# Attention with an FFN before and behind it on one core: order round the first scores and the fourth block, and A11 and A12 of FFN pair 2 turned by DMA

## What is computed

```python
x = L0_attn_x                                   # 2 x 1024 x 512, fp32
x = x + 0.5 * ffn(layernorm(x))
x = x + attention(layernorm(x))
x = x + 0.5 * ffn(layernorm(x))                 # same weights as above
# ffn: (silu(x @ Wg) * (x @ Wu)) @ Wd, 512 -> 1376 -> 512, weights from 4-bit groups
# attention: one head of 128, q k v = x @ Wqkv + b; softmax(q k^T / sqrt(128)) v @ Wo + bo
```

## Time and profile before

| | us |
|---|---|
| median of 3 runs | 828.96 (828.56 to 829.65) |
| the profiled execution | 829.12 |
| its span, first to last instruction | 827.3 |
| TensorE busy in it | 808.2 |

### The profile page before, as it was taken

How to read it: one execution, slowest core, us unless ns; L and a number is a source line. 1 busy time by engine, 2 the same in 40 slices (tenths; PEclk the granted TensorE clock), 3 DMA queues, 4 the chain that set the end, 5 groups by cost and what they waited for, 6 DMA issues and landing times. The chain is left out here.

```text
span 827.3 us, 10465 instructions
## 1 busy us (share of the span) xinstructions
PE 808.2 (98%) x3836; PEld 663.0 (80%) x3836; DVE 493.6 (60%) x801; ACT 273.0 (33%) x469; POOL 297.9 (36%) x235
## 2 busy tenths in 40 slices
PE   5999999999999999999998999999999999999998
PEld 4777778878888888787886888888878788888786
DVE  7899945766554543563756896545347744443452
ACT  3333433455211211432754872121123311211221
POOL 5556614652115363335754362064431210110100
PEclk9999999999999999999999999999999999999999
DMA  5998968975754467348183058735968155344121
GB/s 162 283 336 276 317 190 278 336 267 229 280 184 147 142 216 189 105 140 252 55 222 135 30 188 324 261 127 153 236 190 239 52 195 174 128 155 150 30 103 51
DMA packets 102205, 155.62 MB, mean 188 GB/s; under 512 B 51820, under 2 KB 62756, under 8 KB 97162
## 3 DMA queue, kind: packets, MB, share of 16 engines
q1 hardware_dynamic: 95476, 143.56, 53.5%
q10 hardware_dynamic: 5814, 7.17, 2.5%
q0 software_dynamic: 864, 4.23, 2.0%
HBM read 104.30 MB, written 44.27 MB: 180 GB/s over the span
## 5 line engine op out<-in xcount | busy, mean ns | idle before, releaser
L877 PE MATMUL ps<-blk,ring 128*128 128x512 f32 (+1 forms) x1386 | 320.9, 389 | 0.1
L877 PEld LDWEIGHTS ps<-blk,ring 128*128 128x128 f32 (+1 forms) x1386 | 256.6, 185 | 58.2 <-POOL blk L2274 0.5
L884 PE MATMUL ps<-wd,hT 128*128 128x512 f32 (+1 forms) x1056 | 250.8, 391 | 0.4 <-DVE hT L1768 0.3
L884 PEld LDWEIGHTS ps<-wd,hT 128*128 128x128 f32 (+1 forms) x1056 | 197.2, 188 | 43.1 <-DVE hT L1768 0.7
L2344 POOL TENSOR_TENSOR h<-h,u 128x512 f32<-128x512 f32 (+1 forms) x33 | 42.7, 1295 | 300.0 <-ACT h L1500 300.0
L884 PE MATMUL ps<-xT,wp 128*128 128x512 f32 x480 | 114.7, 395 | 0.1
L884 PEld LDWEIGHTS ps<-xT,wp 128*128 128x128 f32 x480 | 91.5, 191 | 19.8 <-issue 0.3
L1771 DVE TENSOR_TENSOR u<-ps,p1s 128x512 f32<-128x512 f32 (+1 forms) x66 | 45.3, 687 | 95.3 <-PE ps L877 95.3
L1500 ACT ACTIVATE h<-h 128x512 f32<-128x512 f32 (+1 forms) x33 | 20.9, 632 | 177.0 <-DVE h L1771 177.0
L1771 DVE TENSOR_TENSOR h<-ps,p1s 128x512 f32<-128x512 f32 (+1 forms) x33 | 22.8, 691 | 64.1 <-PE ps L877 64.1
L1771 DVE TENSOR_TENSOR u<-ps,u 128x512 f32<-128x512 f32 (+1 forms) x66 | 45.6, 691 | 24.6 <-PE ps L877 23.6
(11 more groups left out here) (139 smaller groups left out, 905.7 us busy)
## 6 DMA issues: line engine op xcount, KB each, us to landing
ring<-wsaved SPq DMA_DIRECT2D x29, 1024.0 KB, 5.1
ring<-wsaved SPq DMA_DIRECT2D x33, 768.0 KB, 4.6
wsaved<-wp SPq DMA_DIRECT2D x10, 1024.0 KB, 4.8
stream<-xres SPq DMA_DIRECT2D x32, 256.0 KB, 2.2
xn<-stream SPq DMA_DIRECT2D x8, 1024.0 KB, 7.1
xres<-stream SPq DMA_DIRECT2D x32, 256.0 KB, 3.8
wfull<-wf ACTq DMA_DIRECT2D x20, 256.0 KB
wsaved<-wp SPq DMA_DIRECT2D x10, 512.0 KB, 5.1
```

Source lines behind the costliest of these rows:

```text
L877: mm = pe.matmul(ps[0:w, bank, :], ring[:, slot, which, a, kt, 0:w], blk[:, which, b, kt, :], start=not onto and kt == 0 and n == 0, stop= ...
L884: mm = pe.matmul(bank_ap, lhs(a), rhs(b), start=first and n == 0, stop=last and n == 2)
```

## The change

- `PLANED` takes in tile 8; the helpers that count planes are made general for it (`of_parity`).
- A11 and A12 of pair 2 come from tile 8's planes: POOL makes them before the first four `add_bias` of sequence 1, SP stores and turns them behind `load_rows(9)`. `turn_ahead(A11)` and `turn_ahead(A12)` leave TensorE, `x11` leaves ACT, and `x_hi`, `x_lo` and `x_sum` read these quarters from `xn` in SBUF, not from PSUM.
- Pair 2's sums come in the order S1, S2, S3, S4, and S3's move behind the last `p_lo`.
- Block 1's V product is cut in two round the first scores, its Q product in two round `turn_p(0, 0)`.
- Tile 7's four transposes are issued together, and `t_hi` and `t_lo` of all its four parts come at the end of sequence 0.
- Scores 6 and 7, `maximum(1, 6)`, `exp(1, 6)` and others move forward in `later_heads`; `ln_apply(8)` goes ahead of `v_bias(3)`.

```diff
-PLANED = (4, 5, 6, 7, 10, 11)
+PLANED = (4, 5, 6, 7, 8, 10, 11)
-TURN_HALVES = tuple((what, kt) for what in (A21, A22, A11, A12) for kt in range(2))
+TURN_HALVES = tuple((what, kt) for what in (A21, A22) for kt in range(2))
-SUM_HALVES = tuple((what, kt) for what in (S1, S3, S2, S4) for kt in range(2))
+SUM_HALVES = tuple((what, kt) for what in (S1, S2, S3, S4) for kt in range(2))
...
+        def by_dma(q, what):
+            return q == 3 or q == 2 and what in (A11, A12)
...
# SP, attention, b == 0 and else
                     store_planes(7)
-                    turn_planes(7, (0, 1))
+                    turn_planes(7)
                 else:
                     sp.wait_ge(s_alo, 4 * KT)
                     load_rows(9, stream, TOKENS + ROWS)
+                    store_planes(8)
+                    turn_planes(8)
...
                     load_residual(k + 1, stream, base + ROWS, [j - 1])
-                    if b == 0 and j > 1:
-                        turn_planes(7, [j])
...
                     if n == NT:
-                        sp.wait_ge(s_turn, turned(2, A12, 1))
+                        sp.wait_ge(s_xlo, split(2, A12, 1))
+                        sp.wait_ge(s_xsum, summed(2, S4, 1))
# TensorE, product_5
-                    if q == 2:
-                        pe.wait_ge(s_xlo, split(q, A12, 1))
-                        pe.wait_ge(s_xsum, summed(q, S4, 1))
# TensorE, qkv_second, b == 0
+                qkv_product(a, 2, (0, 1))
                 pe.wait_ge(s_qkvlo, 3 * a + 1)
                 score(b, 0)
                 score(b, 1)
-                qkv_product(a, 2)
+                qkv_product(a, 2, (2, 3))
+                qkv_product(a, 0, (0, 1))
                 turn_p(b, 0)
-                qkv_product(a, 0)
+                qkv_product(a, 0, (2, 3))
                 turn_p(b, 1)
                 turn_v(a)
# TensorE, later_heads
                 turn_p(1, 4)
-                turn_ahead(A11, 5)
+                score(1, 6)
                 project(1, 2)
                 turn_p(1, 5)
-                score(1, 6)
+                score(1, 7)
                 project(1, 3)
-                pe.wait_ge(s_xlo, split(2, A11, 1))
-                pe.wait_ge(s_xsum, summed(2, S3, 1))
-                pe.wait_ge(s_x21, copied(2, 1, A11))
-                score(1, 7)
                 pv(1, 2)
                 turn_p(1, 6)
-                turn_ahead(A12, 7)
                 project(1, 4)
# ACT, later_heads
                 p_hi(1, 4)
                 x_hi(2, A11, 0)
-                x11(0)
                 x_hi(2, A11, 1)
-                x11(1)
                 scaled(1, 2)
+                exp(1, 6)
                 p_hi(1, 5)
                 scaled(1, 3)
-                sum_hi(2, S3, 0)
-                sum_hi(2, S3, 1)
-                exp(1, 6)
                 exp(1, 7)
...
                 scaled(1, 5)
+                sum_hi(2, S3, 0)
                 heads_hi(1, 3)
+                sum_hi(2, S3, 1)
# ACT, attention
-                if b:
-                    t_hi(3, (2, 3))
                 v_hi(a)
...
                 if b:
+                    ln_apply(8)
                     v_bias(a)
-                    ln_apply(8)
...
                     if g == 3:
                         v_bias(2)
+                        t_hi(3, (0, 1))
                     heads_hi(b, g)
...
+                t_hi(3, (2, 3))
                 scaled(b, QT - 2)
-                t_hi(3, (0, 1))
                 scaled(b, QT - 1)
# DVE, x_sum
-                    if q == 2:
-                        dve.wait_ge(s_x21, copied(2, kt, A11))
-                        a11 = blk_f[:, S2, 1, kt, :]
-                    else:
-                        a11 = turned_tile(A11)
-                    minus(dst, blk_f[:, S1, 1, kt, :], a11).then_inc(s_xsum, 1)
+                    minus(dst, blk_f[:, S1, 1, kt, :], turned_tile(A11)).then_inc(s_xsum, 1)
# DVE, later_heads
                 p_lo(1, 4)
-                for kt in range(2):
-                    x_lo(2, A11, kt)
-                    x_sum(2, S3, kt)
+                maximum(1, 6)
+                x_lo(2, A11, 0)
+                x_lo(2, A11, 1)
                 p_lo(1, 5)
                 inverse(1, 4)
                 inverse(1, 5)
-                maximum(1, 6)
                 maximum(1, 7)
...
                 inverse(1, 7)
+                x_sum(2, S3, 0)
+                x_sum(2, S3, 1)
+                heads_out(1, 3)
                 sum_lo(2, S3, 0)
                 sum_lo(2, S3, 1)
                 x_sum(2, S4, 0)
-                heads_out(1, 3)
                 x_sum(2, S4, 1)
# DVE, attention
-                if b:
-                    t_lo(3, (2, 3))
                 v_lo(a)
...
-                t_lo(3, (0, 1))
+                t_lo(3, range(KT))
# POOL, attention
                 deviation(6 + 2 * b)
                 if b == 0:
                     normalise(6)
+                else:
+                    to_planes(8)
                 add_bias(b, range(RT))
```

More of the change, by code:

```diff
@@ L277, in turn_at @@
             if q == 2:
-                return {A21: 4, A22: 6, A11: 6, A12: 6}[what] + kt
+                return {A21: 4, A22: 6}[what] + kt
             return LOW[q] + (A11, A21, A22, A12).index(what)
@@ L353, in plane_rows, with of_parity @@
             return xn[:, t % 2, r - 1, :].bitcast(U16).rearrange("p (h c) -> p h c", h=2)
+        def of_parity(t):
+            return [u for u in PLANED if u % 2 == t % 2].index(t)
         def planes_made(t, r):
-            return s_planes[t % 2], RT * (PLANED.index(t) // 2) + r + 1
+            return s_planes[t % 2], RT * of_parity(t) + r + 1
         def rows_loaded(t):
@@ L361, in planes_stored @@
         def planes_stored(t):
-            return d_planes[t % 2], 16 * RT * (PLANED.index(t) // 2 + 1)
+            return d_planes[t % 2], 16 * RT * (of_parity(t) + 1)
         def planes_turned(t):
-            return d_xT[t % 2], 16 * KT * (PLANED.index(t) // 2 + 1)
+            return d_xT[t % 2], 16 * KT * (of_parity(t) + 1)
         def turned_rows(t, k):
@@ L386, in split, with copied, block_rows, turned_block @@
             return 6 * (q - 1) + (SPLIT_TILES if q % 2 else SPLIT_HALVES).index((what, kt)) + 1
[L388 to L397, removed]
+        def copied(q, kt):
+            return 2 * (q - 1) + kt + 1
+        def by_dma(q, what):
+            return q == 3 or q == 2 and what in (A11, A12)
+        def block_rows(q, what):
+            return {2: 8, 3: 10}[q] + (what in (A21, A22))
+        def turned_block(q, what, kt):
+            return turned_rows(block_rows(q, what), kt + (2 if what in (A12, A22) else 0))
         def heads_split(a, j):
@@ L1271, in turn_ahead @@
             def turn_ahead(what, j):
-                pe.wait_ge(s_ln[8 + (what in (A21, A22))], RT)
+                pe.wait_ge(s_ln[9], RT)
                 pe.wait_ge(s_exp, QT + j + 1)
@@ L1456, in x21 @@
                 copy(blk_f[:, S3, 1, kt, :], ps[:, turn_at(q, A21, kt), :]).then_inc(s_x21, 1)
-            def x11(kt):
-                copy(blk_f[:, S2, 1, kt, :], ps[:, turn_at(2, A11, kt), :]).then_inc(s_x21, 1)
             def x_hi(q, what, kt):
-                if q == 3:
-                    act.wait_ge(*planes_turned(block_rows(what)))
-                    src = turned_block(what, kt)
+                if by_dma(q, what):
+                    act.wait_ge(*planes_turned(block_rows(q, what)))
+                    src = turned_block(q, what, kt)
                 else:
@@ L1800, in turned_tile @@
                 def turned_tile(which):
-                    if q == 3:
-                        dve.wait_ge(*planes_turned(block_rows(which)))
-                        return turned_block(which, kt)
+                    if by_dma(q, which):
+                        dve.wait_ge(*planes_turned(block_rows(q, which)))
+                        return turned_block(q, which, kt)
                     dve.wait_ge(s_xhi, split(q, which, kt))
@@ L1834, in x_lo @@
                 dve.wait_ge(s_xhi, split(q, what, kt))
-                if q == 2 and what == A11:
-                    dve.wait_ge(s_x21, copied(2, kt, A11))
-                src = turned_block(what, kt) if q == 3 else ps[:, turn_at(q, what, kt), :]
+                src = turned_block(q, what, kt) if by_dma(q, what) else ps[:, turn_at(q, what, kt), :]
                 minus(blk[:, what, 1, kt, :], src, f32(blk[:, what, 0, kt, :])).then_inc(s_xlo, 1)
@@ L2293, in to_planes @@
                         if t >= 6:
-                            pool.wait_ge(*planes_stored(PLANED[PLANED.index(t) - 2]))
+                            pool.wait_ge(*planes_stored(7 if t == 11 else t - 2))
                     else:
```

## The result

| | us |
|---|---|
| changed kernel, median of 5 runs | 833.07 (832.97 to 835.99) |
| kernel before beside it, median of 5 | 828.96 (828.56 to 830.0) |
| ratio | 1.0057, interval 1.0039 to 1.0076 |
| span of the profiled execution | 831.1 (827.3 before) |

The change makes the kernel 4.1 us slower. TensorE is busy for the same 808.2 us as in the earlier trace rows, on 16 instructions fewer: what it saved has come back as a slower clock, and its waits have grown.

A forecast was written before the change was run, and what follows sets the result against it. TensorE, busy 98% of the span, was taken as the bound, so its work, waits or clock decide. -1.25 - 5.1 + 5.4 + 1.0 = 0.05 gave 829.2, said as 828.8 for small credits; range 824.8 to 831.8.

The forecast's parts named there:

- Part 1: First scores of sequence 0: half of V fills the wait on kT; -1.25 us, bounds 0 and -1.56.
- Part 2: Block 3's turned rows: the wait on xT_odd goes, 0.9 on kT stays; -5.1 us, bounds -6.0 and -3.5.
- GpSimd's copies of tile 8: Four copies of 1.04 us ahead of add_bias, in GpSimd's idle time, through at about 452: nothing, bounds 0 and +1.
- Part 3: Heads 4 to 7 of sequence 1: TensorE's saving less new waits, +5.4 us, bounds +1.0 and +7.9.
- (a): Before pv(1, 2): exp(1, 6), maximum(1, 6) and the x_lo(A11) pair stand ahead; wait 2.3 us, from 1.35 to 2.7.
- (c): Before product_7: sum_lo(S3) and x_sum(S4), twice each, stand ahead of middle; wait 3.9 us, bounds 1.7 and 5.6.
- what leaves TensorE: 474.44 to 497.14: two turn_ahead groups go, some 0.9 us each, and other small waits; the stretch shrinks by 2.4.
- rival 4: Full exclusion: six two-operand operations each end with GpSimd's, 1.98 us rather than 1.64; time 830.8, chance 0.05.
- the clock: Slower clock behind the gap at product_7, also at pv: 1.0 us taken, bounds 0 and 3.4.
- rival 2: Clock level falls behind both waits, before pv(1, 2) and product_7, 1.7 us each; time 831.2, chance 0.13.
- (a) to (c): Waits in heads 4 to 7 of sequence 1: 2.3 before pv(1, 2), 0.6 and 1.0 between, 3.9 before product_7.
- product_7 after 500: Sign of mis-sized waits in heads 4 to 7: product_7 starting after 500 or more than 2 us before 497.

The follow-up runs named there:

- part_1: The kernel before with only V and Q of block 1 cut in two round the first scores and turn_p(0, 0): 826.88 us.
- warm: The changed kernel with 9 dummy matmuls before pv(1, 2) and 13 before product_7(2, 0), into a bank nobody reads: 830.23 us.
- narrow: The changed kernel with GpSimd's add_bias (groups 4 to 7) and total (groups 2 to 5) of sequence 1 on 1 column instead of 512: 826.31 us.
- stats_9: The kernel before with the block 1 cuts and tile 7 hunks, plus p_lo(1, 0) ahead of ln_stats(9) on VectorE: 825.95 us.
- reordered: The changed kernel with p_hi(1, 5) ahead of exp(1, 6), x_lo(A11) behind maximum(1, 7) and x_sum(S2, 1), S3's sums ahead of S2's: 827.47 us.
- stores_later: The changed kernel, but SyncE stores tile 8's planes only when tile 9 has been loaded: 834.34 us.
- turn_alone: The changed kernel with later_heads in the order of before, A11 and A12 still turned by DMA and read from SBUF: 828.35 us.
- xlo_late: The changed kernel with the two x_lo(A11) behind p_lo(1, 5) on VectorE instead of ahead of it: 833.34 us.
- parts_1_2: The kernel before with block 1's V and Q cut, tile 7's transposes together and its splits at sequence 0's end: 823.85, again 823.44 us.

## Why the prediction was wrong

**Right.** Part 1: -1.25 forecast; the wait on `kT` is 0.21, and from K of block 1 to the scores of group 2 it is 13.62 us, 1.4 less than before. Part 2: the price, -5.1 with 0.9 left on `kT`, against some -5.2 with 0.26 left. Of the two causes that it names, part_1 and the rows beside it bear out the place behind block 2's work on ScalarE and VectorE; that SP's late transposes held the rows is not borne out. No run leaves the transposes apart and moves the splits alone, so whether issuing them together was needed stays open: the first of the moved copies starts at 429.69, close to the old landing at 429.2. In SP's queue the four transposes go out together and tile 8's load follows at 430.81 (430 to 431 worked out; the earlier trace rows had 427.55):

```profile
413.49 5.18 SPq L646 DMA_TRANSPOSE xn<-planes  x4
...
430.81 0.43 SPq L618 DMA_DIRECT2D xn<-stream  x1
...
442.07 0.43 SPq L618 DMA_DIRECT2D xn<-stream  x1
```

GpSimd's copies of tile 8, put at nothing: it is through at 451.88 (452 forecast) and then waits 1.85 for VectorE. Part 3, all three places and causes: 2.75 before pv(1, 2) (2.3 forecast), 0.53 and 0.45 before project(1, 5) and product_2 (0.3 and part of 1.0), 3.74 before product_7 (3.9). VectorE's and GpSimd's timelines show (a) and (c) as described:

```profile
473.34 1.29 POOL L2394 TENSOR_TENSOR xres<-xres,osb 128x512 f32<-128x512 f32 x1 [5.96 <-ACT osb L1631]
473.38 3.47 DVE L1762 TENSOR_TENSOR blk<-xn,blk 128x512 fp32r<-128x512 f32 x2
...
474.58 1.72 POOL L2389 TENSOR_TENSOR xres<-xres,bo 128x512 f32<-128x512 f32 x1
...
476.77 1.28 DVE L1762 TENSOR_TENSOR pT<-ps,pT 128x512 fp32r<-128x512 f32 x2
...
493.83 2.66 DVE L1762 TENSOR_TENSOR blk<-blk_f,blk 128x512 fp32r<-128x512 f32 x2
...
496.42 2.35 DVE L1762 TENSOR_TENSOR blk_f<-xn,blk_f 128x512 f32<-128x512 f32 x2
...
498.69 0.68 DVE L1765 TENSOR_TENSOR u<-ps,p1s 128x512 f32<-128x512 f32 x1
```

The x_lo pair starts 0.04 us behind a GpSimd operation and takes 3.47 instead of 1.36; each of the two ends about half a microsecond behind the GpSimd operation it met. Then sum_lo(S3) and x_sum(S4) stand 2.66 and 2.35 long ahead of `u` at 498.69. Measured from the turn_p(1, 4) to product_7 in warm, where no clock is lost, part 3 cost 28.70 - 22.70 = 6.0, against +5.4. The waits were not under-priced (7.5 in the changed kernel, 7.8 in the sum); the term that was mis-sized is what leaves TensorE, put at 2.4: 7.5 - 6.0 gives 1.5, and of the two groups the first runs from 475.34 to 476.16 in the earlier trace rows, 0.82 us. The Trainium skill's rule (SBUF — State Buffer, Who interferes with whom), that the later one blocks until the first is done, agrees with these rows and narrow; rival 4, which priced it at 1.98 for each, was too dear, as the median is 1.76.

**The step that failed first: the clock.** I wrote "I take 1.0; bounds 0 and 3.4 (also at pv)". It was 3.4: the level fell behind both gaps, which was rival 2, given 0.13. The gap before product_7 had been put between the two rows and priced at a share of 1.7, but the level either drops, at 1.7, or does not. No row of the kernel before showed a gap of 2 to 3 us alone, so both drops should have stood in the range in full. warm shows this term by itself: 2.8 us in the medians. The sign that was to say that (a) to (c) are mis-sized, product_7 after 500, did not come (499.51): the waits were sized about right and what follows from them was not.

**The second: a wait that had no term.** The prediction says of tile 9's load only "load_rows(9) ... is not delayed". It was not, but TensorE came 6.8 us earlier and the load only 3.2. Before, the load was issued at 445.23 and VectorE read it at 454.63 without a wait:

```profile
445.23 0.37 SPq L612 DMA_DIRECT2D xn<-stream  x1
...
454.63 2.46 DVE L1779 BATCH_NORM_STATS2 stats<-xn 128x6 f32<-128x512 f32 x4
```

After:

```profile
449.49 2.48 DVE L1773 BATCH_NORM_STATS2 stats<-xn 128x6 f32<-128x512 f32 x4 [1.48 <-DMA xn<-stream]
...
451.88 1.27 DVE L1762 TENSOR_TENSOR pT<-ps,pT 128x512 fp32r<-128x512 f32 x2
```

ln_stats(9) is due at 448.0 and waits 1.48 for the load issued at 442.07, and p_lo(1, 0), of which turn_p(1, 1) has need, stands behind it: 1.39 us on TensorE. SP could not issue the load earlier, as four stores and four loads of `xres` stand before it up to 442. With the landing times of the earlier trace rows, 6.5 to 7.2, a load issued then lands at 448.6 to 449.3, so a wait could have been worked out. Of the load I asked only whether it moved, not how far its reader had.

Taken together: 828.8 + 2.4 (clock) + 1.4 (turn_p) + 0.6 (part 3) - 0.5 (front half) = 832.7, against 833.07; the 0.4 taken off the sum for small credits does not show. Either miss alone would have left the time inside the range (831.2 and 830.2); it ended at 831.8, because the two add and only the first was in it, as a rival.

## What to carry to other kernels

When a stage is moved earlier, list every load and every other engine's work that does not move with it, and compare how far each moves with how far its reader does. Before an operand is taken from PSUM into SBUF, look whether GpSimd is busy when VectorE reads it together with another SBUF operand: 0.68 us became 1.76 here, more than the transposes saved. Where a gap can open on TensorE that is longer than any seen to keep the clock (2.0 us here), put the whole price of a clock drop into the range.

## What the runs showed of the hardware

- Each clock drop cost about 1.7 us wherever it came. Gaps up to 2.0 us left the clock at 1.00 in these profiles; gaps of 2.1 (stats_9), 2.3 (reordered, stores_later), 2.6 (turn_alone), 2.75 and 3.7 (changed kernel) were followed by a drop, but the 2.8 of xlo_late was not. The length of the gap alone doesn't decide it, and these runs don't tell what does.
- Dummy matmuls that nobody reads keep the clock up through a wait: 830.23 against 833.07 us.
- VectorE against GpSimd: four subtractions with both operands in SBUF had a median of 1758 ns beside GpSimd's work and 766 where it was narrowed to one column; those with an operand in PSUM stayed at 0.68. GpSimd's own additions took 1.30 us by themselves and 1.72 beside such a subtraction (474.58 in the changed kernel).
- Tile 9's load of 1 MB landed after 5.9 us (part_1) to 8.6 us (turn_alone) from the same place in the program, and the wait behind it was 0.66 in one execution and 1.79 in another of the same kernel (parts_1_2).
